# A Mamba-like block with a ternary feed-forward layer on eight cores: discretization in six parts, weight chunks asked for earlier, a new order behind w2's threshold

## The reference, cut to what matters

```python
# x: (4, 8192, 1024); log_A, B_param, C_param: (64,); W_in (64,1024); W_out (1024,64)
dt = exp(log_dt);  A = -exp(log_A);  Abar = exp(A * dt)
small = abs(A) < 1e-6
frac = where(small, dt, (Abar - 1) / where(small, 1, A));  Bbar = frac * B_param
u = einsum('bld,nd->bln', layernorm(x), W_in)
h_t = h_{t-1} * Abar + u_t * Bbar                      # scan over the 8192 tokens
x = x + einsum('bln,dn->bld', h * C_param, W_out)
# feed-forward: 1024 -> 4096 -> 1024, weights ternary, activations 8 bit
quant_w(w): s = mean|w|;  clip(round(w / s), -1, 1) * s
quant_a(x): sc = 127 / max|x| per token;  clip(round(x * sc), -128, 127) / sc
h = gelu(quant_a(layernorm(x)) @ quant_w(w1).T)
x = x + quant_a(h) @ quant_w(w2).T
```

## Time and profile before

| | us |
|---|---|
| median of 3 runs | 1147.4 (1144.19 to 1147.94) |
| the profiled execution, its own time | 1146.83 |
| its span, core 0 (the slowest) | 1145.3 |
| spans of the other cores | 1135.9 to 1141.5 |
| TensorE busy | 1012.8 (88%) |
| VectorE busy | 733.5 (64%) |
| ScalarE busy | 336.0 (29%) |
| GpSimd busy | 124.1 (11%) |

### The profile page before, as it was taken

The page is one execution under the profiler, slowest core; times in us unless marked ns, Lnnn a source line. Parts: engine busy times, 40 slices in busy tenths (PEclk is TensorE's granted clock), DMA queues, the critical chain, the costliest instruction groups (busy, mean ns, idle before and its releaser), DMA issues.

```text
span 1145.3 us, 14284 instructions; the slowest of 8 cores (1135.9 to 1145.3 us)
## 1 busy us (share of the span) xinstructions
PE 1012.8 (88%) x4644; PEld 448.1 (39%) x4644; DVE 733.5 (64%) x1167; ACT 336.0 (29%) x433; POOL 124.1 (11%) x215
## 2 busy tenths in 40 slices
PE   5792264198999999999999999999999999999995
PEld 2231121043444444444444444444444444444442
DVE  5876485846766666666666666666666666666640
ACT  2236895603122222222222222222222222222110
POOL 1241120111000000000000000000000000000000
PEclk9895687598999999999999999999999999999998
DMA  8979395422443444444444444444444444432241
GB/s 252 337 240 338 138 317 205 101 65 74 95 93 89 93 92 92 92 92 93 93 93 92 92 93 92 92 92 92 93 92 92 92 92 92 93 74 64 63 88 44
DMA packets 212249, 134.95 MB, mean 118 GB/s; under 512 B 197456, under 2 KB 197584, under 8 KB 210128
## 3 DMA queue, kind: packets, MB, share of 16 engines
q1 hardware_dynamic: 200944, 67.98, 29.1%
q0 software_dynamic: 11232, 66.07, 16.9%
HBM read 67.96 MB, written 16.78 MB: 74 GB/s over the span
## 4 chain that ended last, share of the span: by engine, by line
PE 82%; DVE 5%; DMA 4%; ACT 2%; DVEq 2%; issue 2%; ACTq 1%; SPq 1%; POOL 0%; POOLq 0%
PE pout L744 38%; PE pm L710 37%; DMA BIG<-w2t 2%; PE py L692 2%; DMA BIG<-xh 2%; PE pu L722 2%; PE py L693 2%; ACT BIG L341 1%; PE py L732 1%; ACT BIG L336 1%; PE py L733 1%; DVE BIG L599 1%; DVE BIG L604 1%; SPq L188 0%; ACTq L338 0%
## 5 line engine op out<-in xcount | busy, mean ns | idle before, releaser
L710 PE MATMUL pm<-BIG 128*128 128x512 fp8e4 x2048 | 460.8, 386 | 27.3 <-ACT BIG L355 13.4
L744 PE MATMUL pout<-BIG 128*128 128x512 fp8e4 x2048 | 450.2, 381 | 3.1 <-DVE BIG L578 3.1
L710 PEld LDWEIGHTS pm<-BIG 128*128 128x128 bf16 x2048 | 202.7, 99 | 280.3 <-issue 48.1
L554 DVE TENSOR_REDUCE sm<-BIG 128x1 f32<-128x1024 f32 x128 | 155.7, 1219 | 232.1 <-ACT BIG L355 232.1
L744 PEld LDWEIGHTS pout<-BIG 128*128 128x128 bf16 x2048 | 198.5, 98 | 253.1 <-issue 20.2
L355 ACT ACTIVATE BIG<-pm,sm 128x512 f32<-128x512 f32 x256 | 175.1, 687 | 368.5 <-PE pm L710 367.1
L374 ACT CAST hb_s<-h_s 64x128 bf16<-64x128 f32 x32 | 9.5, 298 | 274.3 <-DVEq L519 274.1
L570 DVE TENSOR_SCALAR BIG<-BIG,sm 128x4096 f16<-128x4096 f32 x32 | 75.3, 2352 | 4.6
L270 POOL TENSOR_TENSOR sm<-sm 128x1 f32<-128x1 f32 x32 | 27.5, 858 | 441.7 <-DVE sm L534 441.7
L578 DVE SCALAR_TENSOR_TENSOR BIG<-pout,sm,BIG 128x1024 f32<-128x1024 f32 x32 | 41.1, 1283 | 38.3 <-PE pout L744 32.8
L301 POOL DMA_DIRECT2D out<-BIG x32 | 17.5, 546 | 352.2 <-DVE BIG L578 352.2
(11 more groups left out here) (117 smaller groups left out, 525.8 us busy)
## 6 DMA issues: line engine op xcount, KB each, us to landing
BIG<-xh SPq DMA_DIRECT2D x32, 512.0 KB, 17.7
BIG<-w1t POOLq DMA_DIRECT2D x8, 2048.0 KB, 28.0
BIG<-w2t POOLq DMA_DIRECT2D x8, 2048.0 KB, 21.1
out<-BIG POOLq DMA_DIRECT2D x32, 512.0 KB, 6.5
BIG<-xo POOLq DMA_DIRECT2D x30, 512.0 KB, 3.8
BIG<-BIG SPq DMA_TRANSPOSE x92, 3.1
BIG<-xo SPq DMA_DIRECT2D x2, 512.0 KB, 10.3
BIG<-winT SPq DMA_DIRECT2D x1, 256.0 KB, 13.2
```

The costliest lines, as they stand in the source:

```text
L554: v.tensor_reduce(am4[:, j:j + 1], h_of(c)[:, j * 1024:(j + 1) * 1024], AX.X, ALU.max, apply_absolute_value=True)
L710: m = t.matmul(pm1[G % 3], k1T[c % 2][:, k, :], t1T[gi][:, k, :], start=(k == 0), stop=(k == 7))
L744: i = t.matmul(pout[:, d * 512:(d + 1) * 512], k2T[c % 2][:, m, :], t2T[m // 4][:, m % 4, d * 512:(d + 1) * 512], start=(m == 0), stop=(m ...
```

## The change

- `zoh_b` gets a `part` of 0 to 5, two operations each. The rows' parts run after the statistics of chunks 10 to 15, the column's after those of 20 to 25; `abt` moves behind chunk 26, `winT` behind 17 and `woct` behind 18. The wait for `abar` goes from chunk 8 to chunk 10.
- `load_w1(i)` is issued after the power of chunk 22+i in place of 24+i.
- ScalarE runs one Gelu on a 128x1 tile right behind the gather, ahead of its first `absum`.
- ScalarE's `floor_clip(1, 3)` comes ahead of `gelu(0, 0)`.
- Behind w2's threshold: ScalarE cuts chunks 1, 2, 3, 5, 6, then `xnorm(2)`, chunk 7, `hbf(2)`. VectorE cuts chunks 0 to 3, then `stats(2)`, chunk 4, `hquant(1)`, chunks 5, 6, 7, `scan(2)`. TensorE runs the first 48 matmuls of `mm2(0)` (m below 24, weight chunks 0 to 5) ahead of `mmu(2)`, then the last 16, then `mmy(2)`.

```diff
@@ gpsimd, in the gather
-                if 24 <= c:
-                    load_w1(c - 24)
+                if 22 <= c < 30:
+                    load_w1(c - 22)
@@ scalar
+            s.activation(s1(97), nhalf, AF.Gelu, bias=0.0, scale=1.0)
             absum(0, 4096, wab, "abs1", 1)
...
             floor_clip(1, 2)
+            floor_clip(1, 3)
             gelu(0, 0)
-            floor_clip(1, 3)
             gelu(0, 1)
...
-            for w in (1, 2, 3, 5):
+            for w in (1, 2, 3, 5, 6):
                 floor_clip(2, w)
             xnorm(2)
-            floor_clip(2, 6)
+            floor_clip(2, 7)
             hbf(2)
-            floor_clip(2, 7)
             xnorm(3)
@@ vector: zoh_b(t, pn, bp, part), the same twelve operations, two to a part
-                if c == 8:
+                if c == 10:
                     v.wait_ge(S["abar"], 1)
-                    zoh_b(col, 64, pcol[0:64, 1:2])
+                if 10 <= c < 16:
+                    zoh_b(row, 128, prow[:, N:2 * N], c - 10)
+                if 20 <= c < 26:
+                    zoh_b(col, 64, pcol[0:64, 1:2], c - 20)
+                if c == 26:
                     v.tensor_scalar(abt, ones[0:64, :], col["Abar"], None, op0=ALU.mult)
-                if c == 12:
-                    zoh_b(row, 128, prow[:, N:2 * N])
-                if c == 16:
+                if c == 17:
...
+                if c == 18:
                     v.wait_ge(S["wol"], 16)
@@ vector, behind threshold(2)
-            for w in range(5):
+            for w in range(4):
                 ternary(2, w, t2g)
             stats(2)
+            ternary(2, 4, t2g)
             hquant(1)
             v.tensor_scalar(a2[1], a2[1], s2o, None, op0=ALU.mult)
-            ternary(2, 5, t2g)
+            for w in (5, 6, 7):
+                ternary(2, w, t2g)
             scan(2)
-            ternary(2, 6, t2g)
-            ternary(2, 7, t2g)
             fin(0)
@@ tensor: mm2(c, lo=0, hi=32), waits at lo == 0 only, semaphore at hi == 32 only
             total(2)
+            t.wait_ge(S["ek1"], 2)
+            mm2(0, 0, 24)
             mmu(2)
+            mm2(0, 24, 32)
             mmy(2)
-            t.wait_ge(S["ek1"], 2)
-            mm2(0)
             mm2(1)
```

More of the change, by code:

```diff
@@ L450, in zoh_a, with zoh_b @@
                 v.tensor_scalar(t["lnab"], t["Aneg"], dtc[0:pn, 0:1], None, op0=ALU.mult)
[L452 to L464, removed]
+            def zoh_b(t, pn, bp, part):
+                if part == 0:
+                    v.tensor_scalar(t["am1"], t["Abar"], -1.0, None, op0=ALU.add)
+                    v.tensor_scalar(t["mask"], t["expA"], 1e-6, None, op0=ALU.is_lt); D_()
+                elif part == 1:
+                    v.tensor_tensor(t["d1"], t["mask"], t["Aneg"], ALU.mult); D_()
+                    v.tensor_tensor(t["d1"], t["Aneg"], t["d1"], ALU.subtract); D_()
+                elif part == 2:
+                    v.tensor_tensor(t["den"], t["d1"], t["mask"], ALU.add); D_()
+                    v.reciprocal(t["rden"], t["den"]); D_()
+                elif part == 3:
+                    v.tensor_tensor(t["f0"], t["am1"], t["rden"], ALU.mult)
+                    v.tensor_scalar(t["f1"], t["mask"], dtc[0:pn, 0:1], None, op0=ALU.mult); D_()
+                elif part == 4:
+                    v.tensor_tensor(t["f3"], t["mask"], t["f0"], ALU.mult); D_()
+                    v.tensor_tensor(t["f3"], t["f0"], t["f3"], ALU.subtract); D_()
+                else:
+                    v.tensor_tensor(t["f3"], t["f3"], t["f1"], ALU.add); D_()
+                    v.tensor_tensor(t["Bbar"], t["f3"], bp, ALU.mult); D_()
             zoh_a(row, 128, row["expA"])
@@ L734, in mmy, with mm2 @@
                          stop=True).then_inc(S["y"], 1)
[L736 to L740, removed]
+            def mm2(c, lo=0, hi=32):
+                if lo == 0:
+                    t.wait_ge(S[f"hT{c % 2}"], 16 * (c // 2 + 1))
+                    if c >= 1:
+                        t.wait_ge(S["out"], c)
+                for m in range(lo, hi):
                     if c == 0 and m % 4 == 0:
@@ L746, in mm2 @@
                                      start=(m == 0), stop=(m == 31))
-                i.then_inc(S["mm2"], 1)
+                if hi == 32:
+                    i.then_inc(S["mm2"], 1)
             def turn(src, sem):
```

## The result

The changed kernel takes 1133.32 us, the median of four runs (1132.76 to 1134.57), beside 1145.91 us for the kernel before on the same chip (four runs, 1144.19 to 1147.94). The ratio is 0.9891, its 95% interval 0.9868 to 0.9914. The forecast was 1134 in a range of 1129 to 1141, so the time came out as predicted. Of its two terms, the larger (11.8 us, the front behind w2's threshold) measured 11.0 to 11.2 us, and the smaller (1.45 us, the gather) gave nothing.

The account below looks back on a forecast made before the run. TensorE was taken to bound the kernel (82% of the chain), so the front's gain carries to the end. The terms 1.45 + 0 + 0 + 0 + 11.8 = 13.2 us gave 1134 us, range 1129 to 1141.

Parts of the forecast that it names:

- Discretization: Gather: with VectorE's total work the limit, spreading the operations gains 1.45 us on core 0, near 0.5 on full-clock cores.
- less some 0.3 us of small gaps: Gather, VectorE: the reordered operations end at 79.03 again, some 0.3 us sooner through fewer small gaps.
- 78.7 and 80.4: Gather: signs in the new trace, VectorE's last variance near 78.7 us and TensorE's last group at 80.4.
- Rival C: Gather: short gaps keep TensorE at 1.2 GHz, making the kernel slower, 1165 us; chance 0.06.
- w1 two chunks sooner: Up to w1's threshold: issue at about 61 us in place of 67, gain 0 by itself, a cover for a shorter gather.
- no wait for data at VectorE's half of the last sum: Sign at L583, before w1's threshold: the 8.42 us DMA wait goes, as w1 lands some 5 us sooner.
- ScalarE's two edits: Before w2's threshold: chunk 3 begins 3.5 us sooner, but the wait for w2 grows to about 10; gain 0.
- Behind w2's threshold: mm2(0) begins at 214.8 in place of 227.22 and ends at 232.1 in place of 243.86: gain 11.8 us.
- the clock's start: TensorE, mm2(0): 2.7 us added to its first 48 matmuls for starting at the low clock.
- B: mm2(0) gets half its gain, through a low clock for most matmuls or a late chunk: 1140 us; chance 0.14.
- D: Behind 265 us something other than TensorE paces the blocks, so the gain is given back: about 1146; chance 0.06.
- E: w2's landing moves with the cut chunks, or the gather gives the 6 us after all: 1130; chance 0.08.

Follow-up runs that it names:

- e10: Changed kernel with the discretization's twelve operations replaced by one each time (Abar - 1 in Bbar's place, other output): 1127.76 us, ratio 0.9859.
- e1: Kernel before with only the new orders behind w2's threshold, on VectorE, ScalarE and TensorE: 1133.73 us, ratio 0.9897.
- e7: Kernel before with only the first half of each w2 chunk loaded, plus ScalarE's two edits (other output): 1135.86 us, ratio 0.9917.
- e3: Kernel before with only ScalarE's two edits, the early Gelu and floor_clip(1, 3) ahead of gelu(0, 0): 1146.23 us, ratio 1.0008.
- e2: Kernel before with only the discretization in six parts and w1 asked for two chunks sooner: 1146.13 us, ratio 1.0006.
- e4: Kernel before with only TensorE's order, 48 matmuls of mm2(0) ahead of mmu(2) and 16 behind it: 1141.15 us, ratio 0.9961.
- e5: Kernel before with only VectorE's and ScalarE's new orders behind w2's threshold, TensorE as before: 1149.61 us, ratio 1.0038.
- e8: Changed kernel with mm2(1) split as mm2(0) is, and what mmu(3) needs moved forward on the other queues: 1127.16 us, ratio 0.9834.
- e9: e4 with ScalarE's new order too (floor_clip(2, 7) ahead of hbf(2)), VectorE as in the kernel before: 1136.81 us, ratio 0.9937.

## Why the prediction was right, and where it was not

**Discretization: 1.45 us predicted, none found.** This is the step that failed. Its limit was the right one, VectorE's sum (e10), but three things in the term were too large. It took "less some 0.3 us of small gaps"; with the operations in six parts the same sequence took 0.27 longer instead (why is not shown; the number of operations and drains is the same). It took a row of core 0, where the half clock had left TensorE 0.94 us further behind VectorE than on the seven others. And the last group begins 1.73 us behind the last variance (78.70 to 80.43), not 1.66. So even core 0 had only 1.45 - 0.57 - 0.07 = 0.8 us to gain, and the others, where "near 0.5" had been predicted, lost 0.1. The kernel after shows it on VectorE and then TensorE:

```profile
26.75 0.69 DVE L483 BATCH_NORM_STATS2 sm<-BIG 128x6 f32<-128x512 f32 x1 [3.92 <-DMA BIG<-xh]
...
78.70 0.15 DVE L488 TENSOR_SCALAR sm<-sm 128x1 f32<-128x1 f32 x1
```

```profile
46.07 1.04 PE L701 MATMUL py<-BIG,pch 128*64 128x512 f32 x2 [0.31 <-ACT pch L327]
...
53.39 1.04 PE L701 MATMUL py<-BIG,pch 128*64 128x512 f32 x2 [0.81 <-ACT pch L327]
...
80.43 1.05 PE L701 MATMUL py<-BIG,pch 128*64 128x512 f32 x2
```

78.70 and 80.43 are the very numbers that the prediction asked for, 78.7 and 80.4. They are no confirmation. Chunk 8 landed at 26.75 on this core and at 27.36 in the earlier trace rows, so VectorE took 51.95 us here and 51.67 there. An absolute time is only worth something beside the event that started it.

**Rival C.** The short stops are there, ten of them from chunk 14 on (0.23 to 0.81 us), and every pair of matmuls behind them takes 1.04 or 1.05 us. At the half clock it was 1.94. The window from 30 to 60 us shows clock 0.94 on core 4; what is missing from 1.00 follows the stop of 3.07 us for chunk 8 (the pair at 31.44 takes 1.92). The seven other cores show 1.00. Before, two cores had 1.00, five 0.94 and core 0 the 0.83 of the earlier trace rows. The rule of the Trainium skill that spoke against the change (TensorE: Matmul & The Clock Gate, A second HAM failure mode: psum-queue depth-cycling) is not borne out by these rows; stops of this length left the clock alone.

**w1 two chunks sooner: 0, right.** It was issued from 61.29 us on. The sign that was named, no wait for data at VectorE's half of the last sum, did not come: the wait fell from 8.42 us to 3.14 here, and is 2.4 to 4.9 on the eight cores.

```profile
115.26 2.29 DVE L592 TENSOR_REDUCE sm<-BIG 128x1 f32<-128x2048 f32 x1 [3.14 <-DMA BIG<-w1t]
```

It ends nothing, as ScalarE's half begins only at 122.14. The stage to total(1) is 42.3 us with the edit, and 42.3 in e1 without it. The 42.4 of before comes from two cores on which w1's landing did reach the threshold (42.95 us on core 6 and 42.50 on core 7, 42.26 on the rest). As a cover for a shorter gather the edit was not put to use, since the gather did not shorten.

**ScalarE's two edits: 0, right, with the size hidden behind it wrong.** Its wait for w2 went from 5.5 to 8.0 us in the mean, not "to about 10", because the edits save 2.5 and not 3.5 (e7). The table load stands at 80.12, and none is left at L355.

**Behind w2's threshold: 11.8 us.** The table gives 11.0 at the end of mm2(0) and 11.1 at mm1(2) in the mean, and on the slowest core of each profile 48.3 and 37.1 us from total(2), 11.2. The 0.8 us that are missing are in two places. The start gained 12.2 us (31.7 to 19.5 behind total(2)) where 12.4 had been counted. And from its first matmul to its last, mm2(0) became 1.2 us longer in the mean over the cores (16.3 to 17.4) where 0.6 had been counted (16.64 to 17.2, with core 0's time for before). Its end came nearly right although one term did not: the clock's start, counted as 2.7 us, cost 1.4 on core 4 (the first eight matmuls take 3.24, the later eights 1.89) and 1.5 to 3.0 on the others. Where it cost less, the stops for weight chunks 5 and 7 took up most of the rest, so that mm2(0) takes 17.14 to 17.59 us on all cores. The prediction had found these two limits to agree, and that made the size of this term matter little.

The stop for fin(0) is 1.00 us, not the 1.54 that was carried over; the 0.5 us did not reach mm1(2), which waits for its transpose. mmu(2) took its turn at 225.13 without a wait. B, a cold start for most of mm2(0), is refuted by the durations: 40 matmuls in 10.15 us is 0.25 each, the eights behind them take 1.89, and on no core are more than 14 of the 64 slow. D is refuted by the window. Of E, the first half is refuted (w2's landing did not move, e3), and the second too: six microseconds are in the gather, but only for who removes the work.

**The sum.** 13.2 predicted; the medians differ by 12.6 and the mean spans by 11.7. The total was nearer than its parts, and that is luck: beside the 1145.1 us that the kernel before takes in the runs of e1, the difference is 11.8. The slowest cores of the two profiles (1145.3 and 1133.0) differ by 12.3 us: 11.3 of that is the front up to mm1(2), 1.4 the gather, and the rest, -0.4, the other stages (1.1 up to w2's threshold, -1.5 behind mm1(2)). The gather's 1.4 is core 0's half clock and the landing of its first data more than the change, since e2, which has the same gather, shows no gain at all.

## What to carry to other kernels

Here work cut into smaller pieces on a full engine gave nothing: ask first whether the engine is short of time in sum or only at one moment, and size a stall's removal by what the engine behind it owes in total. An order across engines is one edit: from total(2) to mm1(2) e4 alone gains 4.9 us and e5 loses 5.1, and together (e1) they gain 11.3, because every engine must leave the small chain (mmu, scan, hbf, mmy) at the same place. Small links of the next block belong inside the large matmul group ahead, on all queues.

## What was not expected of the hardware

GpSimd's power for stats(2), a tile of 128 x 1, in the kernel after:

```profile
211.00 4.64 POOL L261 TENSOR_TENSOR sm<-sm 128x1 f32<-128x1 f32 x1 [6.25 <-DVE sm L518]
```

Before, with only small operations on VectorE beside it:

```profile
217.83 0.56 POOL L261 TENSOR_TENSOR sm<-sm 128x1 f32<-128x1 f32 x1 [10.56 <-DVE sm L509]
```

Begun at 211.00, it ended at 215.64. VectorE's two passes over weight chunk 4, shown above, ran from 210.88 to 215.60 with 0.08 us between them.

The runs settle what it depends on. It takes 4.64 or 4.65 us on every core of the five runs in which VectorE has stats(2) ahead of chunk 4 (the kernel after, e1, e5, e8, e10), and 0.56 on every core of the seven others. e9 and e1 differ in VectorE's order alone, and it is 0.56 in e9 and 4.64 in e1. So what makes it long is VectorE's order, which puts the passes beside it.

The Trainium skill (SBUF — State Buffer, Who interferes with whom) says that GpSimd shares its ports with VectorE's second pair, and that a VectorE operation which uses that pair holds it until it ends. The rows agree with that, in that the operation, begun 0.12 us behind the first pass, ended 0.04 us behind the second; that it is the ports is not shown by a run here.

It cost nothing, because xnorm(2) at 216.29, after 2.40 us of waiting for it, still left mmu(2)'s input in time: its transpose was asked for at 217.7 and landed 3.1 us later, at 220.8, for a mmu(2) at 225.13.

```profile
216.29 1.24 ACT L367 ACTIVATE BIG<-BIG,sm 128x1024 bf16<-128x1024 f32 x1 [2.40 <-POOL sm L263]
```

The prediction gave this link no time of its own and did not say what stands beside it on VectorE. In an order without slack it would have cost up to 4.64 - 0.56 = 4.1 us, which is an estimate from the two rows.
